# Two reorderings in the Gelu steps of a two-network kernel: the third up product, and one copy of turned probabilities

## What is computed

```
h = shift_token(x)                     # half of the channels from the token before
q, k, v = split(h @ wqkv)              # 8 heads of 64
q = l2norm(q) * qs;  k = l2norm(k) * ksc
q, k = rotary_xpos(q, k)
o = local_attention(q, k, v)           # windows of 64, each sees itself and the one before
x = x + o @ wo
h = layernorm(shift_token(x)) * lg + lb
a, g = split(h @ w1 + b1)              # 341 hidden channels each
x = x + (a * gelu(g)) @ w2 + b2
```

## Time and profile before

| | us |
|---|---|
| median of 3 runs | 2159.86 |
| lowest and highest of them | 2158.65, 2161.14 |
| the profiled execution | 2162.79 |
| its span, first to last instruction | 2161.0 |
| TensorE busy | 2070.8 |
| VectorE busy | 1825.5 |
| ScalarE busy | 1673.6 |
| GpSimd busy | 1389.0 |

### The profile page before, as it was taken

One profiled execution on the slowest core, in us unless ns is written; L12 is line 12 of the kernel. 1 busy time (PEld: TensorE's weight loads), 2 busy tenths in 40 slices (PEclk: granted clock), 3 DMA queues, 4 the chain that ended last, 5 costly groups with the idle time before them and its releaser, 6 DMA issues. The chain is left out here.

```text
span 2161.0 us, 87976 instructions
## 1 busy us (share of the span) xinstructions
PE 2070.8 (96%) x33646; PEld 1430.2 (66%) x33646; DVE 1825.5 (84%) x4867; ACT 1673.6 (77%) x5828; POOL 1389.0 (64%) x1318
## 2 busy tenths in 40 slices
PE   7989999999999999999999999999999788999998
PEld 4656766667666666666666666666666565666665
DVE  5889988888988889898888889888896587888873
ACT  4767888888888888888888888888887336787784
POOL 1337867777776777777677777767774226666660
PEclk9999999999999999999999999999999988999999
DMA  4001222112211222112221222112221100000000
GB/s 119 5 3 37 76 62 50 46 52 67 61 44 46 72 61 51 43 48 72 63 50 45 53 67 61 44 46 63 50 52 37 31 18 6 14 16 13 15 11 25
DMA packets 144805, 97.03 MB, mean 45 GB/s; under 512 B 61976, under 2 KB 137408, under 8 KB 144384
## 3 DMA queue, kind: packets, MB, share of 16 engines
q1 hardware_dynamic: 143232, 91.02, 16.6%
q10 hardware_dynamic: 1152, 0.26, 0.1%
HBM read 23.11 MB, written 1.05 MB: 11 GB/s over the span
## 5 line engine op out<-in xcount | busy, mean ns | idle before, releaser
L726 PE MATMUL bank<-wqkv,hs 128*128 128x512 f32 x1344 | 658.3, 610 | 5.0 <-ACT arena L1581 2.5
L1972 POOL TENSOR_TENSOR arena<-arena,rnorm 128x512 f32<-128x512 f32 x448 | 455.3, 1045 | 277.7 <-DVE rnorm L259 276.4
L1965 POOL TENSOR_TENSOR arena<-arena 128x512 f32<-128x512 f32 x448 | 565.9, 1273 | 58.0 <-DVE arena L2185 58.0
L1610 ACT ACTIVATE arena<-bank,amx 128x64 f32<-128x64 f32 x1536 | 457.5, 332 | 26.7 <-DVE amx L2242 26.4
L726 PEld LDWEIGHTS bank<-wqkv,hs 128*128 128x128 f32 x1344 | 230.2, 191 | 178.1 <-issue 158.1
L1610 ACT ACTIVATION_READ_ACCUMULATOR arena<-bank,amx 128x1 f32 x1536 | 346.3, 225 | 0.0
L2185 DVE TENSOR_TENSOR arena<-bank,rot 128x256 f32<-128x256 f32 x896 | 334.2, 415 | 0.0
L2180 DVE TENSOR_TENSOR arena<-bank,rot 128x512 f32<-128x512 f32 x448 | 306.7, 685 | 23.6 <-PE bank L726 20.8
L1587 ACT ACTIVATE arena<-bank 128x512 f32<-128x512 f32 x426 | 249.9, 621 | 87.9 <-PE bank L747 87.9
L747 PEld LDWEIGHTS bank<-ident,arena 128*128 128x128 f32 x1792 | 213.3, 142 | 155.4 <-issue 112.4
L1979 POOL TENSOR_TENSOR arena<-arena,ainv 128x512 f32<-128x512 f32 x192 | 200.2, 1043 | 167.7 <-DVE ainv L2250 167.5
(11 more groups left out here) (229 smaller groups left out, 3290.2 us busy)
## 6 DMA issues: line engine op xcount, KB each, us to landing
arena<-arena SPq DMA_DIRECT2D x768, 64.0 KB
wqkv<-in_L_ffn_Wqkv_dram SPq DMA_DIRECT2D x24, 256.0 KB
hs<-z SPq DMA_DIRECT2D x128, 32.0 KB, 2.1
hs<-z SPq DMA_DIRECT2D x128, 31.8 KB, 1.9
fx<-z SPq DMA_DIRECT2D x31, 128.0 KB, 2.2
fx<-z SPq DMA_DIRECT2D x31, 127.0 KB, 2.5
wqkv<-in_L_ffn_Wqkv_dram SPq DMA_DIRECT2D x24, 128.0 KB
w<-in_L_ffn_W_dram SPq DMA_DIRECT2D x6, 341.0 KB
```

The costliest lines, as they stand in the source:

```text
L726: nc.tensor.matmul(bank[o][:], src[:], wqkv[w][:, off:off + 512], start=True, stop=True).then_inc(AT[name] if part < 2 else AT[name][i], 1)
L1610: ins = nc.scalar.activation(pb[i][0][p % 2][:, h * DH:(h + 1) * DH], bank[3 + g][:, j * DH:(j + 1) * DH], ACT.Exp, bias=amx[p % 2][:, i, ...
L1965: nc.gpsimd.tensor_tensor(t, t, rs[i][c], ALU.add).then_inc(AT["ak" if c else "aq"][i], 1)
L1972: nc.gpsimd.tensor_tensor(t, t, rnorm[p % 2][:, i, HU * c:HU * c + HU].unsqueeze(2).to_broadcast([P, HU, DH]), ALU.mult).then_inc(AT["mk" ...
```

## The change

It makes two moves, both only in steps with c = 1. On TensorE, slot 4 of the feed-forward part, which is the third up product there, is called ahead of the two turns of unit 1 (keys and queries), right behind the value projection `project_in(1, s - 2, 2, 7, "v")`. On ScalarE, the copy `probs(1, s - 2, 1)`, which stood behind both halves of the exponentials, is called between the first half and the second; `probs(1, s - 2, 0)` stays behind both. The steps with c = 0 keep their order, and no instruction is added or removed.

```diff
--- before.py
+++ after.py
@@ -1145,6 +1145,9 @@
                         else:
                             at(pe, AT["ve"][0], s - 1)
                         project_in(1, s - 2, 2, 7, "v")
+                    gelus = ff_phase(ph, s)[0] == 1
+                    if gelus:
+                        feed_forward_1(s, 4)
                     if live(s - 1):
                         if live(s - 2):
                             at(pe, AG["pte"][1][1], nth(1, s - 2))
@@ -1156,7 +1159,8 @@
                         else:
                             at(pe, AT["qte"][0], s)
                         turn(1, s - 1, 0, "mq", "qt")
-                    feed_forward_1(s, 4)
+                    if not gelus:
+                        feed_forward_1(s, 4)
                     if live(s - 2):
                         at(pe, AT["ve"][1], s - 1)
                         values(0, s - 2)
@@ -1742,9 +1746,13 @@
                         ff_gelu(f)
                     if live(s - 1):
                         exponents(0, s - 1, 1)
+                    if live(s - 2) and c == 1 and f >= 0:
+                        probs(1, s - 2, 1)
+                    if live(s - 1):
                         exponents(0, s - 1, 0)
                     if live(s - 2):
-                        probs(1, s - 2, 1)
+                        if not (c == 1 and f >= 0):
+                            probs(1, s - 2, 1)
                         probs(1, s - 2, 0)
                     if live(s):
                         square(1, s, 0)
```

## The result

The changed kernel takes 2167.83 us (median of 6 runs, 2165.37 to 2169.51), the kernel before 2160.50 us beside it: ratio 1.0024, 95% interval 1.0014 to 1.0035, so slower by 5.2 us (3.0 to 7.6). The two medians lie 7.3 us apart, near the upper end of that interval; this text goes by the ratio. Forecast were 2165.1 us, with a range of 2161.5 to 2168.5. The profiled execution after took 2165.37 us.

The account below looks back on a forecast made before the run. TensorE, busy 96% of the span, was taken to bound the kernel. Five Gelu steps of 0.86 us and one of 0.87 gave +5.2 us; on the 2159.86 us median, 2165.1 us (+0.24%), range 2161.5 to 2168.5.

Parts of the forecast that it names:

- The copy: On ScalarE in Gelu steps: the moved copy of probabilities puts four exponentials back by 0.48 us, bounds 0.48 and 0.61.
- The product: On TensorE: the third up product waits for its bank 2 to be read out; values(0) begins 0.66 us late.
- the tile: VectorE's second hidden tile, read out of bank 2 behind the exponentials and reciprocal; ends at 1941.02 instead of 1940.54.
- The turned keys and queries: ScalarE's copies wait for TensorE's late turns, so unit 1's scores start at 1944.20 instead of 1943.34, 0.86 us late.
- smaller than it looks: Rival: only TensorE's own delay counts, 6 x 0.66 = 4.0 us, giving 2163.9 us, within 0.2%; chance 0.20.
- The faster rival: Rival: the product fills TensorE's gap and the turns find the copy done, -4.0 us, 2155.9 us; chance 0.10.
- The clock: Forecast: no clock loss in five regular Gelu steps. Rival: it falls there, +12.5 us in all, 2172.4 us; chance 0.08.
- the last step: Gelu step s = 112, without projections of a next pair: +0.87 us, bounds -0.6 and +2.3 for the half clock.
- The step's 0.86 us: Delay of unit 1's scores in each of the five regular Gelu steps, taken as the loss per step.
- the release of the mask products: Time from the end of ScalarE's turned queries to TensorE's first score products, taken as 0.05 us.
- 18 Gelus of full width: Count in the forecast: 18 such Gelus, three to a step, hence six Gelu steps.

Follow-up runs that it names:

- after, queries first: Changed kernel with ScalarE's turned queries of unit 1 ahead of the square in Gelu steps; two-step pitch 42.54 us against 42.94, no ratio given.
- values first: Product, tile and queries early, plus ScalarE's value copy and turned tiles ahead of both squares, third hidden tile ahead of its sums; ratio 0.9975 to the kernel before.
- after, one wait: Changed kernel, but in Gelu steps TensorE waits before unit 1's scores only for the turned queries; two-step pitch 42.75 us against 42.94, no ratio given.
- copy alone: Changed kernel with the third up product back behind the turns, so only ScalarE's copy is moved; ratio 1.0006 to the kernel before, pitch 42.28 us.
- product alone: Changed kernel with ScalarE's copy back in its old place, so only the third up product is moved; ratio 1.0021 to the kernel before, pitch 42.45 us.
- product, tile and queries: Kernel before with third up product ahead of the turns, second hidden tile ahead of VectorE's reciprocal, turned queries ahead of ScalarE's square; ratio 0.9989, pitch 41.38 us.
- copy alone, queries first: Kernel before with ScalarE's copy moved and its turned queries of unit 1 put ahead of the square in Gelu steps; pitch 42.29 us, no ratio given.

## Why the prediction was right, and where it was off

**The copy** put the four exponentials back by 0.48 us, as forecast. **The product** waits for the tile and starts 3.15 us after the passes (forecast 3.13). **The turned keys and queries** are late because ScalarE's three copies are in one queue: "after, queries first" takes back 0.46 us of it, so the rival *smaller than it looks* falls. **The faster rival** falls with the tile: the product does fill the gap, but only in the kernels in which the tile is early. **The clock** stays at 1.00 in the regular steps through a gap of 1.4 us (1.27 in the bracket, which counts the modelled ends of the passes). The forecast took that from the gap of the earlier trace rows, and there it had some luck. All twelve kernels have that gap; behind it the clock stayed at 1.00 in eleven, and fell in the kernel with the values first:

```profile
1848.69 0.66 PE L814 MATMUL bank<-ident,arena 128*128 128x128 f32 x4 [1.43 <-ACT arena L1591]
```

```profile
1850.00:1851.00 1.00, 1.00 (x24) 0.99 (x18) 0.00 (x0) 0.10 (x1) 1.00 (x2) 0.50 0.00 0
```

So a kept clock behind one gap is no proof for the next of the same length. The Trainium skill's rule of a clock lost at every burst (TensorE: Matmul & The Clock Gate, section "HAM oscillation — how this bites in real kernels") is not what the regular steps show. The case in that section of the Trainium skill has longer waits than any gap here; even so the last step lost the clock in or right behind gaps of 2.0 to 2.9 us in six of the seven kernels that have one.

**Mis-sized terms.** The step's 0.86 us measured 1.13. The term that was mis-sized is the release of the mask products, taken at 0.05 us from the chain's turns: it is 0.25, and 0.05 once the waits around it are gone ("after, one wait"). The same row of waits was in the kernel before, so its 0.2 should have come off both sides; I took the old start from the record, in which it was contained, and the new one from a sum, in which it wasn't. The remaining 0.07 us were there before ScalarE's copies: the product starts 0.02 us later than forecast, and from its start to the turns it is 0.92 us where I took 0.86. That the ratio gives just the forecast 5.2 us is chance: the rows give 6.2, the medians 7.3. In the last step I took +0.87 and it was +0.58, in this execution. The first work there starts 0.88 us later, as forecast. The half clock lasts as long as before (before, the stretches from 2108 to 2112 have 0.51, 0.50, 0.50 and 0.78; after, those from 2111 to 2115 have 0.61, 0.50, 0.50 and 0.69), but it now begins 0.6 us ahead of the first work instead of behind it, so less work lies under it. Where the low stretch falls was luck: with the same gap it was absent in one kernel and twice as long in another. Together 5 x 0.27 - 0.29 = +1.1 us, so 5.2 becomes 6.2 (6.3 by these rounded terms). The "18 Gelus of full width" are 12 of 128 partitions and 6 of 85; there are six Gelu steps either way.

**Missed.** I priced the copy only through the tile. Without the product's move it costs 0.47 us a step by a chain that I had not followed: rotation, norms, GpSimd, the turns of the next step. In the kernel after that chain is late too (GpSimd's scaling at 10.17 us, so a bound of 12.83 at line 902, an estimate from the copy alone) and is hidden by TensorE's own 13.58. It did not change the forecast, but whoever undoes the product alone finds it. And I named a saving in the last step as a bound only; the copy alone makes it, in both kernels that have it without the product's move.

The two halves of the edit work against each other in the last step. The gaps show it: 2.00 us with neither, 2.39 with the product alone, 2.87 with both, and with the copy alone 0.60 and 1.23 with four turns between. The copy's turns would have cut the gap, but the product stands ahead of them and waits. The times were 7.61, 7.96 (2112.28 to 2120.24), 8.19 and 5.98 us; how much of their differences the clock makes varies from one execution to the next.

**Open.** The kernel with product, tile and queries should gain 4.5 us by its rows, a little more than its interval holds; where the difference goes was not found. Outside the Gelu steps single executions differ by more than that: by up to 6.8 us ahead of the first, and by up to 2.0 us behind the last; half-clock stretches that come and go are part of it. No run here shows how often they come. How much of f_b's stretch below is the port and how much is order was not separated. Nor was the copy's move tried together with all three others.

## What to carry to other kernels

A move ahead of a wait only pays if what is moved is ready: read on the record what its own bank is released by, and move that releaser first (here one VectorE tile; it turned a loss of 1.13 us a step into 0.04). After one edge is gained, expect the next chain within tenths of a microsecond, and look for it over the step boundary and in the engines that look idle. A piece of work that cuts a long gap of TensorE in two can be worth more than the work it hides, if the gap costs the clock.

## What the runs showed of the hardware beside that

**The clock.** Gaps of TensorE in or right behind which the granted clock fell to 0.50 (1.2 GHz): 1.43 us (values first), 2.0 (before and two more kernels), 2.4 (product alone), 2.9 (after, and after with queries first). Kept at 1.00: 0.60 and 1.23 us with four turns between them, 0.92 behind two passes, 1.27 in all regular steps of the three kernels with both moves and the late tile, 1.43 in eleven kernels, and 2.88 (after, one wait). So the length of a gap alone doesn't decide.

**VectorE beside GpSimd.** Timeline of VectorE before, in the step above and the next:

```profile
1943.81 0.62 DVE L2221 TENSOR_SCALAR n_s<-ss 128x32 f32<-128x32 f32 x1
1944.47 0.96 DVE L248 TENSOR_SCALAR ny<-n_s 128x32 int32<-128x32 int32 x1
...
1957.09 0.89 DVE L250 TENSOR_TENSOR f_b<-fy,f_s 128x4 f32<-128x4 f32 x1
```

These small operations end 0.02 to 0.04 us after GpSimd's running one in its rows above: 1944.43 against 1944.39, 1945.43 against 1945.40, 1957.98 against 1957.96. The same operation of line 250 takes 0.16 us where GpSimd is idle (1958.60, before), and 0.97 in "copy alone, queries first", where GpSimd's operation ends at 1957.98 and f_b at 1957.99, later against the mask products (4.57 us, before 4.49). The turn of line 877 behind it moves from 5.73 to 5.82: this is the 0.09 of the stretch "to passes". The Trainium skill (SBUF — State Buffer, section "SBUF: two separate sides") says that VectorE and GpSimd hold a shared pair of ports by turns, and that the one that comes second stands until the first is done; these rows agree with it, though no run here took GpSimd's operation away.
